# The opening of a time-mix kernel rebuilt, and the rows of its last eight tiles given places of their own

## The chip, the cores and the metric

One Trainium2 chip, one of its cores. The metric is the device time of one execution in microseconds, the median of several.

## What is computed

The reference, cut to what matters: x is (4, 1024, 512), which is 32 tiles of 128 rows, 8 tiles for each batch.

```python
mod = (silu(c) @ wmod).reshape(4, 6, 1, 512)          # c is (4, 512), wmod (512, 3072)
sa, ca, ga, sb, cb, gb = (mod[:, i] for i in range(6))
ga, gb = [(2 * (g >= 0) - 1) * maximum(abs(g), 0.25) for g in (ga, gb)]
h = layernorm(x) * (1 + ca) + sa
# attention part on h: layernorm with ln1, shift by one row, three mixes with mu_r, mu_k, mu_v
r, k, v = sigmoid(xr @ Wr.T), xk @ Wk.T, xv @ Wv.T
h = h + (r * exp(u + k) * v / (exp(u + k) + 1e-8)) @ Wout.T
h = h + sigmoid(xr2 @ Wr2.T) * (square(relu(xk2 @ Wk2.T)) @ Wv2.T)   # second layernorm, shift, mixes
x = x + ga * h
h = layernorm(x) * (1 + cb) + sb
# 8 experts, the best 2 of each row, and a shared one: silu(h @ Wg.T) * (h @ Wu.T) @ Wd.T
x = x + gb * (routed(h) + shared(h))
```

## The kernel before

Each matrix is used as a high part and a low part (`w_r_hi`, `w_r_lo`), and each product of 128 rows and 512 columns is 12 matmuls: four chunks of the inner dimension, by high times high, low times high and high times low. ACT makes the high part of a weight by a copy (`split_hi`), DVE the low part by a subtraction (`split_lo`).

The order is written out by hand for each engine, and semaphores tie the engines together. In the time mix (the first of the two attention parts), step t works on several tiles at once: DVE reads the statistics of x for tile t+4 (`x_stats`), forms h for tile t+3 (`scaled`, `h_of`), normalises tile t+2 (`hhat`) and mixes tile t+1 (`first_col`, `mixes`, `mix_lo`). PE multiplies tile t by r, k and v, turns tile t+2 (`t1`), and from step 2 on turns and multiplies tile t-2 by o. DVE adds that result in `x2_of`. The first steps are -4 to -1, in which PE has nothing of r, k or v to do. POOL forms the reciprocal roots and the difference of neighbouring rows (`diff`). In SP's queue stand the loads of x, the stores of h (`store_h`), and the loads that bring h back. The two places for h are used in turn, so `h_of` of tile n waits until the store of tile n-2 has landed.

Ahead of the time mix stands the opening. PE multiplies silu(c) with the six columns of wmod (24 matmuls, 4 rows each), and each row goes from PSUM to SBUF on DVE, five operations for each gate. The rows are stored to HBM (`store_mod`) and loaded again, spread over 128 partitions, for each batch (`mod1`). The seven weights of the two attention parts pass through three staging buffers and are split, the last three (r2, k2, v2) in the first steps but ahead of tile 0's product.

Behind the attention parts come the experts, in units of 24 matmuls (gate and up, 352 columns) and 9 (down, 512 columns). Units 30 to 37 belong to the shared expert, unit 38 is the first routed one. Rows go to the experts by a scatter of POOL into `expert_in_rows`. SP loads the rows of tiles 24 to 31 for it, writes eight pieces of zeros behind the experts' rows (`pad_rows`, each from the third on waits for the one two before), loads the first two experts' weights (`load_gu`, `load_dn`) and then the first rows (`load_rows`), after all scatters and zeros have landed. PE turns these (`turn_rows(0)`) in unit 37.

## Time and profile before

| | us |
|---|---|
| median of 3 runs | 1725.35 |
| lowest and highest of them | 1723.52, 1727.61 |
| the profiled execution, its own time | 1726.2 |
| span of the profiled execution | 1724.5 |
| PE busy in it | 1642.5 |

The span runs from the first to the last instruction of the core, and the own time of the execution has 1.7 us around it. Times within the trace count from the start of the span. PE is the engine of the matmuls, DVE the vector engine, ACT the scalar engine, POOL the one that scatters, SP the one that issues most transfers. A matmul in the trace lasts longer than the distance to the next one, since they overlap: the distance is what a matmul costs.

### The profile page before, as it was taken

What the parts mean: (1) busy time and instruction counts of PE and PEld (TensorE: products, weight loads), DVE (VectorE), ACT (ScalarE), POOL (GpSimd) and SP (SyncE); (2) the same over time, 40 slices, a digit from 0 to 9 for tenths busy, and PEclk for the clock granted to TensorE, in tenths of its full rate; (3) what the DMA queues carried; (4) which work ended last, traced back from release to release, by engine and by line L of the source; (5) the groups of instructions that cost most, each with busy time, mean ns of one, the idle gap of its engine ahead of it and who ended that gap; (6) DMA issues with size and microseconds to landing.
All of it is one profiled execution on the core that took longest, in us unless ns stands there. A gap on an engine that the chain in (4) does not pass through costs nothing.

```text
span 1724.5 us, 26984 instructions
## 1 busy us (share of the span) xinstructions
PE 1642.5 (95%) x8813; PEld 1429.8 (83%) x8813; DVE 1329.4 (77%) x2559; ACT 766.8 (44%) x1132; POOL 414.3 (24%) x504
## 2 busy tenths in 40 slices
PE   5399999999989999999999997999999999999998
PEld 0278888888768888888888886999999999998897
DVE  4799999998689788888788773777777777775872
ACT  2343333334445555464545422555555555552321
POOL 0243444444222111322232341000000000005740
PEclk9699999999999999999999998999999999999999
DMA  8443232221454434555555687888878988776861
GB/s 327 111 155 98 73 97 79 91 91 67 166 167 146 166 141 141 194 192 196 195 185 177 226 283 260 268 290 283 284 266 277 299 293 282 258 237 194 283 213 37
DMA packets 139121, 335.82 MB, mean 195 GB/s; under 512 B 20584, under 2 KB 20584, under 8 KB 133376
## 3 DMA queue, kind: packets, MB, share of 16 engines
q1 hardware_dynamic: 109328, 248.65, 43.6%
q10 hardware_dynamic: 19440, 52.18, 8.3%
q0 software_dynamic: 10240, 33.56, 5.6%
q8 instruction: 62, 1.02, 0.2%
q14 instruction: 51, 0.42, 0.1%
HBM read 230.73 MB, written 103.60 MB: 194 GB/s over the span
## 4 chain that ended last, share of the span: by engine, by line
PE 78%; DVE 10%; DMA 5%; issue 3%; POOL 2%; ACT 2%; SPq 1%; DVEq 0%; ACTq 0%; POOLq 0%
PE bank L687 19%; PE bank L689 19%; PE bank L688 19%; PE bank L698 5%; PE bank L2321 5%; PE bank L2319 5%; PE bank L2320 5%; PE bank L2314 2%; DMA stage<-in_w_k 1%; DVE mix L1729 1%; POOL raw L1262 1%; DMA expert_in_rows<-y_rows 1%; DVE xm_lo L1735 1%; PE bank L2303 1%; DMA ex_x<-expert_in_rows 1%
## 5 line engine op out<-in xcount | busy, mean ns | idle before, releaser
L687 PE MATMUL bank<-gu_hi,ex_x_hl 128*128 128x352 f32 x1080 | 361.3, 335 | 0.1
L689 PE MATMUL bank<-gu_hi,ex_x_hl 128*128 128x352 f32 x1080 | 350.1, 324 | 0.0
L688 PE MATMUL bank<-gu_lo,ex_x_hl 128*128 128x352 f32 x1080 | 350.1, 324 | 0.0
L1262 POOL DMA_INDIRECT raw<-expert_out_rows,out_slots x64 | 77.1, 1204 | 540.0 <-DMA expert_out_rows<-y_rows 518.2
L687 PEld LDWEIGHTS bank<-gu_hi,ex_x_hl 128*128 128x128 f32 x1080 | 205.1, 190 | 0.4 <-issue 0.3
L688 PEld LDWEIGHTS bank<-gu_lo,ex_x_hl 128*128 128x128 f32 x1080 | 205.1, 190 | 0.0
L689 PEld LDWEIGHTS bank<-gu_hi,ex_x_hl 128*128 128x128 f32 x1080 | 204.7, 190 | 0.0
L1824 DVE TENSOR_TENSOR hid<-bank,sg_t 128x352 f32<-128x352 f32 x135 | 70.4, 521 | 124.8 <-PE bank L689 106.1
L2319 PE MATMUL bank<-dn_hi,hid_hi 128*128 128x512 f32 x405 | 161.3, 398 | 2.4 <-DVE hid_lo L1828 2.4
L2321 PE MATMUL bank<-dn_hi,hid_lo 128*128 128x512 f32 x405 | 159.6, 394 | 0.0
L2320 PE MATMUL bank<-dn_lo,hid_hi 128*128 128x512 f32 x405 | 158.5, 391 | 0.0
L1379 ACT ACTIVATE hid_hi<-bank 128x384 fp32r<-128x384 f32 x135 | 65.3, 484 | 148.8 <-PE bank L2314 148.8
L2090 DVE TENSOR_TENSOR gu_lo<-raw,gu_hi 128x2816 fp32r<-128x2816 f32 x42 | 129.5, 3083 | 1.7 <-ACT gu_hi L1472 1.7
L1828 DVE TENSOR_TENSOR hid_lo<-bank,hid_hi 128x384 fp32r<-128x384 f32 x135 | 74.5, 552 | 70.5 <-ACT hid_hi L1379 70.2
L1472 ACT ACTIVATE gu_hi<-raw 128x2816 fp32r<-128x2816 f32 x42 | 107.6, 2562 | 43.9 <-PE bank L689 43.9
L1476 ACT ACTIVATE dn_hi<-raw 128x1536 fp32r<-128x1536 f32 x42 | 62.5, 1489 | 127.5 <-PE bank L2321 127.5
L1319 ACT ACTIVATE h2T<-bank,vecs 128x128 f32<-128x128 f32 x128 | 48.1, 458 | 155.0 <-PE bank L698 155.0
L687 PE MATMUL bank<-w_r_hi,xm_hi 128*128 128x512 f32 x256 | 104.8, 409 | 11.4 <-DVE h1T L1654 10.3
L687 PE MATMUL bank<-w_k_hi,xm_hi 128*128 128x512 f32 x256 | 104.9, 410 | 0.0
L1663 DVE SCALAR_TENSOR_TENSOR stage<-diff,vecs,h1T 128x128 f32<-128x128 f32 x384 | 102.9, 344 | 0.0
L688 PE MATMUL bank<-w_r_lo,xm_hi 128*128 128x512 f32 x256 | 101.8, 398 | 0.0
L689 PE MATMUL bank<-w_r_hi,xm_lo 128*128 128x512 f32 x256 | 101.6, 397 | 0.0
(256 smaller groups left out, 3826.3 us busy)
## 6 DMA issues: line engine op xcount, KB each, us to landing
raw<-in_ex_gu SPq DMA_DIRECT2D x40, 1408.0 KB, 6.5
raw<-in_ex_dn SPq DMA_DIRECT2D x40, 512.0 KB, 4.9
ex_x<-expert_in_rows SPq DMA_DIRECT2D x71, 256.0 KB, 6.2
expert_out_rows<-y_rows ACTq DMA_DIRECT2D x71, 256.0 KB, 5.9
h_rows<-h_t SPq DMA_DIRECT2D x64, 256.0 KB, 2.6
h_turned<-h_hl ACTq DMA_DIRECT2D x32, 512.0 KB, 3.0
ex_x_hl<-h_turned ACTq DMA_DIRECT2D x32, 512.0 KB, 3.9
x_t<-in_x SPq DMA_DIRECT2D x32, 256.0 KB, 2.7
```

What stands on the lines that cost most here:

```text
L687: pe.matmul(acc, act_hi[i], w_hi[i], start=(i == 0), stop=False)
L688: pe.matmul(acc, act_hi[i], w_lo[i], start=False, stop=False)
L689: last = pe.matmul(acc, act_lo[i], w_hi[i], start=False, stop=(i == chunks - 1))
L698: last = pe.transpose(bank[:, c * P:(c + 1) * P], rows[:, c * P:(c + 1) * P], ident[:])
L1262: pool.indirect_dma_start(rows[:, pair % 2, a, :], None, ys_d, bass.IndirectOffsetOnAxis(ap=out_slots[:, k, n:n + 1], axis=0)).then_inc(ar ...
L1472: act.activation(flat(gu_hi[j % 2][:]), raw[j % 2][:, 0:C * GU], ACT.Copy).then_inc(rw_hi_act.sem, 1)
L1663: last = dve.scalar_tensor_tensor(mix1[:, m, c, :], diff1[:, c, :], vecs[:, mu, c:c + 1], h1T[:, t.p, c, 0:P], ALU.mult, ALU.add)
L1828: dve.tensor_tensor(flat(hid_lo[:]), PS_H[:, 0:FK * P], flat(hid_hi[:]).bitcast(F32), ALU.subtract).then_inc(u_vec.sem_of["hid_lo"], 1)
L2090: dve.tensor_tensor(flat(w_lo[j % 2][:]), raw[j % 2][:, cols], flat(w_hi[j % 2][:]).bitcast(F32), ALU.subtract).then_inc(rw_lo_vec.sem, 1)
L2319: pe.matmul(PS_Y[:], hid_hi[:, c, :], dn_hi[w][:, c, :], start=start and c == 0, stop=False)
L2320: pe.matmul(PS_Y[:], hid_hi[:, c, :], dn_lo[w][:, c, :], start=False, stop=False)
L2321: last = pe.matmul(PS_Y[:], hid_lo[:, c, :], dn_hi[w][:, c, :], start=False, stop=stop and c == FK - 1)
```

## The change

The opening is put together in another way. The product of ones (1 x 128) with the first batch's row of SA and of CA spreads these over the partitions in PSUM, and ACT copies both to `mod1`; only batches 1 to 3 go by HBM. Rows of SA, CA, SB and CB are copied by ACT, and the two gates are formed by four operations of DVE each, in steps 1 and 3. A weight is loaded into the place of its own low part (`weight_in`), so no staging buffer has to come free. Splits of r and k come ahead of everything, v's in step -2, o's in step 0, and r2, k2 and v2 in steps 5, 8 and 11. The nine vectors are loaded from ACT's queue, and the first two tiles of x are loaded near the front of SP's. PE's products for SB, CB and GB stand in steps -2 and -1. On the other side, rows of tiles 24 to 31 all have places in `base`, the second half of the zeros goes behind the first expert's weights, the second expert's weights behind the first rows, and `turn_rows(0)` behind the gate and up of unit 37.

```diff
...
         for w in W2:
-            hi[w], lo[w] = w2_shelf.put(f"w_{w}_hi", [P, C, D], F32R), w2_shelf.put(f"w_{w}_lo", [P, C, D], F32R)
+            hi[w] = w2_shelf.put(f"w_{w}_hi", [P, C, D], F32R)
+            weight_in[w] = Shelf(nc, w2_shelf.at).put(f"w_{w}_in", [P, C, D])
+            lo[w] = w2_shelf.put(f"w_{w}_lo", [P, C, D], F32R)
...
+        mod_home = Shelf(nc, first.at)
+        sa_rows, ca_rows = mod_home.put("sa_rows", [P, D]), mod_home.put("ca_rows", [P, D])
...
+        LAST_HOME = {24: 7, 25: 8, 26: 0, 27: 1, 28: 2, 29: 3, 30: 5, 31: 6}
+
         def last_rows(n):
 
-            return base[:, n - 26, :] if n < 30 else sc_rows[:, n % 2, :]
+            return base[:, LAST_HOME[n], :]
...
+        MOD_BANK = {SA: psum[0], CA: psum[1], GA: psum[3], SB: psum[4], CB: psum[5], GB: psum[7]}
+        MOD_TURN = {SA: 1, CA: 2, GA: 5, SB: 6, CB: 7, GB: 8}
+        SPREAD_TURN = {SA: 3, CA: 4}
+        MOD_COPIED = {SA: 1, CA: 2, SB: 5, CB: 6}
+        SPREAD = psum[6:8]
+        SPLIT_IN_STEP = {-4: ["r", "k"], -2: ["v"], 0: ["o"], 5: ["r2"], 8: ["k2"], 11: ["v2"]}
+        GATE_IN_STEP = {1: GA, 3: GB}
+        SPLITS_DONE = 12
...
             sp.dma_start(cT[:], io["cT"].rearrange("(c p) b -> p c b", p=P)).then_inc(c_in, 16)
+            sp.dma_start(x_t[:, 0, :], x_d[0:P, :]).then_inc(x_in[0], 16)
             load_wmod(0)
-            load_weight(0)
-            load_weight(1)
+            load_weight("r")
+            load_weight("k")
+            sp.dma_start(x_t[:, 1, :], x_d[P:2 * P, :]).then_inc(x_in[1], 16)
             load_wmod(1)
+            load_weight("v")
             load_wmod(2)
-            for t in range(2):
-                sp.dma_start(x_t[:, t, :], x_d[t * P:(t + 1) * P, :]).then_inc(x_in[t], 16)
-
-            store_mod(0)
-            store_mod(1)
-            for i in range(2, len(W1)):
-                load_weight(i)
-            sp.wait_ge(mod_out, 32)
-            for b in range(B):
-                sp.dma_start(flat(mod1[:, b]), mod_d[b, 0:2 * D].partition_broadcast(P)).then_inc(mod1_in, 16)
-            for m in range(2, 6):
-                store_mod(m)
-            for i in range(len(W1), NW - 1):
-                load_weight(i)
+            load_weight("o")
+            sp.dma_start(u_bc[:], io["u"].partition_broadcast(P)).then_inc(u_in, 16)
+            for m in (SA, CA):
+                sp.wait_ge(mod_act, MOD_COPIED[m])
+                store_mod(m, mod_out)
             sp.wait_ge(*lnh_vec.done(0, "scaled"))
             sp.dma_start(x_t[:, 0, :], x_d[2 * P:3 * P, :]).then_inc(x_in[0], 16)
-            sp.dma_start(u_bc[:], io["u"].partition_broadcast(P)).then_inc(u_in, 16)
-            sp.dma_start(wrt[:], io["wrT"].rearrange("(c p) e -> p c e", p=P)).then_inc(vec_in, 16)
...
+            sp.wait_ge(mod_out, 32)
+            for b in range(1, B):
+                sp.dma_start(flat(mod1[:, b]), mod_d[b, 0:2 * D].partition_broadcast(P)).then_inc(mod1_in, 16)
+
+            def later_mod(t):
+
+                if t.only(0):
+                    sp.wait_ge(mod_act, MOD_COPIED[CB])
+                    store_mod(SB, mod_out)
+                    store_mod(CB, mod_out)
+                    sp.wait_ge(mod_mm, MOD_TURN[GB])
+                    for w in W2:
+                        load_weight(w)
...
             wait_a2(sp)
-            for n in range(24, 26):
-                load_scattered(n)
-            for n in range(26, 30):
+            for n in range(24, NT):
                 load_last_scattered(n)
...
             for e in range(E // 2):
                 pad_rows(e)
-            for n in range(30, NT):
-                sp.wait_ge(sc_out[n % 2], 32 * 13)
-                load_last_scattered(n)
-            for e in range(E // 2, E):
-                pad_rows(e)
             sp.wait_ge(raw_pad, 2)
             sp.wait_ge(route_done, 1)
             load_gu(0)
             load_dn(0)
+            for e in range(E // 2, E):
+                pad_rows(e)
             for n in range(FU + 2, SPLIT):
                 load_residual(n)
-            sp.wait_ge(route_vec, SHIFTS_AT)
-            load_gu(1)
-            load_dn(1)
 
...
             sp.wait_ge(h3T_out, 16 * NT)
             for p in range(2):
                 sp.wait_ge(pad_out[p], 16 * (E // 2))
-                sp.wait_ge(sc_out[p], 32 * 13)
-            sp.wait_ge(sc_last_out, 32 * (NT - 26))
-
-            for k in range(3):
+                sp.wait_ge(sc_out[p], 32 * 12)
+            sp.wait_ge(sc_last_out, 32 * (NT - 24))
+
+            for k in range(2):
                 load_rows(k)
+            sp.wait_ge(route_vec, SHIFTS_AT)
+            load_gu(1)
+            load_dn(1)
+            load_rows(2)
...
+            def split_hi(w):
+                act.wait_ge(*weight_arrived(w))
+                act.activation(flat(hi[w][:]), flat(weight_in[w][:]), ACT.Copy).then_inc(wsplit_hi, 1)
+
...
+            def first_batch(m):
+                act.wait_ge(mod_mm, SPREAD_TURN[m])
+                act.activation(mod1[:, 0, m, :], SPREAD[m][:], ACT.Copy).then_inc(mod_act, 1)
+
             act.wait_ge(c_in, 16)
             act.activation(cT[:], cT[:], ACT.Silu).then_inc(silu_c, 1)
...
+            for i in (G1, B1, MUR, MUK, MUV):
+                load_vector(i)
+            split_hi("r")
+            mod_row(SA)
+            split_hi("k")
+            mod_row(CA)
+            for m in (SA, CA):
+                first_batch(m)
+            act.wait_ge(vec_in, 80)
+            for i in (G2, B2, MUR2, MUK2):
+                load_vector(i)
+            act.dma_start(wrt[:], io["wrT"].rearrange("(c p) e -> p c e", p=P)).then_inc(vec_in, 16)
+
+            def opening(t):
+
+                if t.only(-2):
+                    split_hi("v")
+                if t.only(-1):
+                    mod_row(SB)
+                    mod_row(CB)
+                    split_hi("o")
+                for step, weights in SPLIT_IN_STEP.items():
+                    if step > 0 and t.only(step - 1):
+                        for w in weights:
+                            split_hi(w)
...
-                if u == ROUTED0 - 1:
-                    routed_x_hi(0)
                 for piece in HI_FIRST[u]:
                     expert_hi(*piece)
...
+            routed_x_hi(0)
...
+            def split_lo(w):
+                dve.wait_ge(wsplit_hi, split_at(w))
+                dve.tensor_tensor(flat(lo[w][:]), flat(weight_in[w][:]), flat(hi[w][:]).bitcast(F32),
                                   ALU.subtract).then_inc(wsplit_lo, 1)
 
-            def mod_row(m):
-                dve.wait_ge(mod_mm, m + 1)
-                step = MOD_AT[m - 1] if m else 0
...
-            SA, CA, GA, SB, CB, GB = range(6)
-            split_lo(0)
-            split_lo(1)
-            mod_row(SA)
-            mod_row(CA)
-            mod_row(GA)
-            split_lo(2)
-            mod_row(SB)
-            mod_row(CB)
-            mod_row(GB)
-            split_lo(3)
+            def gate_row(m):
+
+                bank, rows = MOD_BANK[m][0:B, :], mod_rows[m]
+                step = GATE_OPS * (m == GB)
+                dve.wait_ge(mod_mm, MOD_TURN[m])
+                if m == GB:
+                    dve.wait_ge(mod_out, 80)
+                    dve.wait_ge(mod_vec, GATE_OPS)
+                dve.tensor_scalar(rows, bank, 0.0, 2.0, ALU.is_ge, ALU.mult).then_inc(mod_vec, 1)
+                dve.tensor_scalar(gate_size, bank, -1.0, 0.25, ALU.mult, ALU.max).then_inc(mod_vec, 1)
+                dve.wait_ge(mod_vec, step + 2)
+                dve.tensor_tensor(gate_size, bank, gate_size, ALU.max).then_inc(mod_vec, 1)
+                dve.wait_ge(mod_vec, step + 3)
+                dve.scalar_tensor_tensor(rows, rows, -1.0, gate_size, ALU.add, ALU.mult).then_inc(mod_vec, 1)
+                dve.wait_ge(mod_vec, step + 4)
...
+            def opening(t):
+
+                if t.pair is not None:
+                    return
+                for w in SPLIT_IN_STEP.get(t.offset, ()):
+                    split_lo(w)
+                if t.offset in GATE_IN_STEP:
+                    gate_row(GATE_IN_STEP[t.offset])
+                if t.only(-1):
+                    dve.wait_ge(u_in, 16)
+                    dve.tensor_scalar(u_bc[:], u_bc[:], LN_1E8, None, ALU.add).then_inc(u_ready, 1)
...
+                if t.only(0):
+                    dve.wait_ge(mod_act, SPREAD_TURN[CA])
+                elif t.only(TPB):
+                    dve.wait_ge(mod1_in, 16 * (B - 1))
...
+            _, _, first_stages = in_turn(
+                (first_col, -1), (hhat, -2), (scaled, -3), (h_of, -3), (h_stats, -3), (h_moments, -3),
+                (x_stats, -4), (x_moments, -4), (mixes, -1), (mix_lo, -1))
+
+            def time_step(t):
+                if t.pair is None and t.offset < 0:
+                    first_stages(t)
+                else:
+                    later_stages(t)
+                opening(t)
...
+            for m in (SA, CA):
+                mod_product(m)
+            for m in (SA, CA):
+                pe.wait_ge(mod_act, MOD_COPIED[m])
+                pe.matmul(SPREAD[m][:], ones_row, mod_rows[m][0:1, :], start=True, stop=True).then_inc(mod_mm, 1)
+            mod_product(GA)
+
+            def opening(t):
+
+                if t.only(-2):
+                    mod_product(SB)
+                if t.only(-1):
+                    mod_product(CB)
+                    pe.wait_ge(mod_act, SPREAD_TURN[CA])
+                    mod_product(GB)
...
-                elif u == ROUTED0 - 1:
-                    turn_rows(0)
                 turn_hid(u - 1)
                 up(u)
+                if u == ROUTED0 - 1:
+                    turn_rows(0)
```

On DVE the first rows of the program were these (weights' low parts, rows of the modulation, then the statistics of the first tiles):

```order
L1554 TENSOR_TENSOR w_r_lo<-stage_95,w_r_hi 128x2048 [waits wsplit_hi]
L1554 TENSOR_TENSOR w_k_lo<-stage_96,w_k_hi 128x2048 [waits wsplit_hi]
L1571 TENSOR_SCALAR h_t<-bank 4x512 [waits mod_mm] x2
L1563 TENSOR_SCALAR xh<-bank 4x512 [waits mod_vec,mod_mm]
L1564 TENSOR_SCALAR diff_90<-bank 4x512
L1566 TENSOR_SCALAR xh<-xh 4x512 [waits mod_vec]
L1567 TENSOR_TENSOR diff_90<-bank,diff_90 4x512
L1569 TENSOR_TENSOR hh<-xh,diff_90 4x512 [waits mod_vec]
```

From step -2 to the mixing of tile 0 in step -1 they are now these:

```order
L1658 BN_STATS st_111<-x_t 128x6 [waits x_in0]
L763 COPY bridge_col<-eps 128x1 [waits lnx_vec]
L1662 BN_AGGR mv_112<-st_111 128x2
L1618 TENSOR_TENSOR w_v_lo<-w_v_in,w_v_hi 128x2048 [waits wsplit_hi]
L1705 TENSOR_TENSOR h1T<-h1T,keep 128x4
L1699 TENSOR_SCALAR hh<-h_t,mv1h,rstd1h 128x512 [waits lnh_pool]
L1672 SCALAR_TENSOR_TENSOR xh<-x_t,mv_112,mod_94 128x512 [waits lnx_vec]
L1683 SCALAR_TENSOR_TENSOR h_t<-xh,rstd_113,mod_94 128x512 [waits lnh_vec,lnx_pool,h_out0]
L1689 BN_STATS st1h<-h_t 128x6 [waits lnh_vec]
```

The rows of the modulation have left DVE's front. Tile 0's mixing stands behind the statistics of tile 2's x and behind tile 2's h, which waits for the store of tile 0's h (`h_out0`).

In SP's queue, at the way into the routed part, there stood this after the first four pieces of zeros:

```order
L987 DMA sc_rows<-h_rows 128x512 x2
L1025 TENSOR_LOAD pad_row
L1025 ISA x2
L1026 ISA
L1026 DMA expert_in_rows<-y_rows 128x512
```

There stands this now, in which the first expert's weights precede the fifth piece of zeros:

```order
L766 DMA raw_188<-in_ex_gu 128x2816
L771 ISA
L771 DMA raw_188<-in_ex_dn 128x2x512
L773 ISA
L773 DMA raw_188<-in_ex_dn 96x512
L1049 TENSOR_LOAD pad_row
L1049 ISA x2
L1050 ISA
L1050 DMA expert_in_rows<-y_rows 128x512
```

On PE the first routed rows were turned ahead of unit 36's turn (`hid`) and unit 37's 24 matmuls of gate and up:

```order
L2321 MATMUL bank<-dn_hi,hid_lo 128x512
L698 MATMUL bank<-ident,ex_x 128x128 [waits ex_in0]
L698 MATMUL bank<-ident,ex_x 128x128 x3
L2314 MATMUL bank<-ident,hid 128x128 [waits u_vec_hid,u_vec_hid_lo]
L2314 MATMUL bank<-ident,hid 128x128 x2
L687 MATMUL bank<-gu_hi,ex_x_hl 128x352 [waits u_vec_hid]
```

They are turned now behind the last of these 24 and ahead of unit 36's down:

```order
L703 MATMUL bank<-gu_hi,ex_x_hl 128x352
L712 MATMUL bank<-ident,ex_x 128x128 [waits ex_in0]
L712 MATMUL bank<-ident,ex_x 128x128 x3
L2410 MATMUL bank<-dn_hi,hid_hi 128x512 [waits u_vec_hid_lo,base_vec]
L2411 MATMUL bank<-dn_lo,hid_hi 128x512
```

## Rows read from the trace of the kernel before

**Rows 1.** The page of the profile, engines' busy time, share of the span and instructions.

```profile
PE 1642.5 (95%) x8813; PEld 1429.8 (83%) x8813; DVE 1329.4 (77%) x2559; ACT 766.8 (44%) x1132; POOL 414.3 (24%) x504
```

**Rows 2.** Waits of PE: who waited for what, us in total, times, longest.

```profile
PE bank L698 <- DVE hh L1648: 20.4, 1, 20.4
PE bank L698 <- DMA ex_x<-expert_in_rows: 12.2, 1, 12.2
...
PE bank L687 <- DVE h1T L1654: 10.3, 2, 9.6
PE bank L698 <- ACT h1T L1284: 6.3, 1, 6.3
```

**Rows 3.** Timeline of PE, opening: start, us, engine, line, operation, tiles, count.

```profile
9.40 9.88 PE L2194 MATMUL bank<-wmod,cT 128*4 128x512 f32 x16 [9.40 <-DMA wmod<-in_wmod]
20.62 13.90 PE L2194 MATMUL bank<-wmod,cT 128*4 128x512 f32 x32 [1.34 <-DMA wmod<-in_wmod]
...
73.10 0.76 PE L687 MATMUL bank<-w_r_hi,xm_hi 128*128 128x512 f32 x1 [9.64 <-DVE h1T L1654]
...
105.32 0.40 PE L687 MATMUL bank<-w_r_hi,xm_hi 128*128 128x512 f32 x1
```

**Rows 4.** Chain that ended last, opening, transfers: start us, us, what.

```profile
4.04 11.42 DMA stage<-in_w_k
...
21.22 8.55 DMA stage<-in_w_v
```

**Rows 5.** Windows (busy per engine, PEclk, DMA share, GB/s) of the vector loads.

```profile
42.00:56.00 14.00, 1.05 (x4) 0.72 (x4) 9.97 (x17) 3.82 (x2) 2.13 (x7) 0.50 0.76 176
```

**Rows 6.** Timeline of DVE, opening, idle time in brackets.

```profile
24.25 0.68 DVE L1563 TENSOR_SCALAR xh<-bank 4x512 f32<-4x512 f32 x1 [3.35 <-PE bank L2194]
...
50.68 2.29 DVE L1554 TENSOR_TENSOR w_k_lo<-stage,w_k_hi 128x2048 fp32r<-128x2048 f32 x1 [2.28 <-ACT w_k_hi L1275]
...
60.23 0.69 DVE L1609 BATCH_NORM_STATS2 st<-x_t 128x6 f32<-128x512 f32 x1 [3.70 <-DMA x_t<-in_x]
...
66.41 3.24 DVE L1663 SCALAR_TENSOR_TENSOR stage<-diff,vecs,h1T 128x128 f32<-128x128 f32 x12
...
71.20 1.76 DVE L1669 TENSOR_TENSOR xm_lo<-stage,xm_hi 128x1536 fp32r<-128x1536 f32 x1 [0.67 <-ACT xm_hi L1292]
72.87 0.16 DVE L1654 TENSOR_TENSOR h1T<-h1T,keep 128x4 f32<-128x4 f32 x1
...
82.39 0.16 DVE L1654 TENSOR_TENSOR h1T<-h1T,keep 128x4 f32<-128x4 f32 x1
...
92.97 0.15 DVE L1654 TENSOR_TENSOR h1T<-h1T,keep 128x4 f32<-128x4 f32 x1
...
103.84 0.15 DVE L1654 TENSOR_TENSOR h1T<-h1T,keep 128x4 f32<-128x4 f32 x1
```

**Rows 7.** Timeline of DVE, ten tile steps later.

```profile
224.66 0.15 DVE L1654 TENSOR_TENSOR h1T<-h1T,keep 128x4 f32<-128x4 f32 x1
```

**Rows 8.** Waits of DVE, 112 to 400 us.

```profile
DVE hin_t L1694 <- PE bank L689: 18.5, 24, 0.9
```

**Rows 9.** Timeline of PE where the routed part begins.

```profile
1051.63 0.39 PE L2321 MATMUL bank<-dn_hi,hid_lo 128*128 128x512 f32 x1
1064.18 1.11 PE L698 MATMUL bank<-ident,ex_x 128*128 128x128 f32 x4 [12.17 <-DMA ex_x<-expert_in_rows]
...
1070.04 0.32 PE L687 MATMUL bank<-gu_hi,ex_x_hl 128*128 128x352 f32 x1
...
1071.47 0.39 PE L2319 MATMUL bank<-dn_hi,hid_hi 128*128 128x512 f32 x1
```

**Rows 10.** Timeline of SP's queue, the same place.

```profile
1052.83 1.45 SPq L1063 DMA_DIRECT2D ex_x<-expert_in_rows  x2
```

**Rows 11.** Transfers, 1015.25 to 1064.2 us, all queues.

```profile
DMA packets 5941, 15.64 MB, mean 320 GB/s; under 512 B 752, under 2 KB 752, under 8 KB 5682
```

**Rows 12.** Transfers of rows of zeros, 1037 to 1046 us: count, KB, us to landing.

```profile
expert_in_rows<-y_rows SPq DMA_DIRECT2D x4, 256.0 KB, 3.5
```

More of the change, by code:

```diff
@@ L236, in put, with time_mix @@
         return tensor
-def time_mix(eng, lead, lag, body):
-    low = lag + 2 + lag % 2
+def time_mix(eng, lead, lag, body, low=None):
+    low = low or lag + 2 + lag % 2
     high = min(NT - lead, JOIN) // 2 * 2
@@ L545, in build @@
         u_in = sem("u_in")
-        w_in = [sem(f"w_in{i}") for i in range(3)]
+        w_in = [sem(f"w_in{i}") for i in range(len(W1))]
         mod_out = sem("mod_out")
@@ L1245, in scatter_last @@
                                             last_rows(n), None).then_inc(sc_last_out, 16)
-            for n in range(24, 26):
-                scatter(n)
-            for n in range(26, NT):
+            for n in range(24, NT):
                 scatter_last(n)
@@ new lines, in opening @@
+            def opening(t):
[9 more added lines that the diff above has]
+                            split_hi(w)
+                if t.only(SPLITS_DONE - 2):
+                    act.wait_ge(vec_in, 160)
+                    act.activation(wrt_hi, wrt[:], ACT.Copy).then_inc(wsplit_hi, 1)
@@ L2187, in _, with mod_product @@
         def _(pe):
-            pe.wait_ge(silu_c, 1)
-            for m in range(6):
-                if m % 2 == 0:
-                    pe.wait_ge(wmod_in[m // 2], 16 * C)
+            def mod_product(m):
+                pe.wait_ge(wmod_in[m // 2], 16 * C)
                 for c in range(C):
-                    last = pe.matmul(psum[m][0:B, :], cT[:, c, :], wmod[:, c, m * D:(m + 1) * D], start=(c == 0),
+                    last = pe.matmul(MOD_BANK[m][0:B, :], cT[:, c, :], wmod[:, c, m * D:(m + 1) * D], start=(c == 0),
                                      stop=(c == C - 1))
                 last.then_inc(mod_mm, 1)
+            pe.wait_ge(silu_c, 1)
             pe.wait_ge(const_ready, CONSTS)
-            pe.wait_ge(mod_vec, MOD_DONE)
+            for m in (SA, CA):
[11 more added lines that the diff above has]
+                    mod_product(GB)
             def t1(t):
@@ L2212, in r @@
                     pe.wait_ge(*sr_act.done(t.back(1).n, "sr"))
-                if t.pair is None and t.n == 0:
-                    pe.wait_ge(wsplit_lo, NW + 1)
+                if t.only(0):
+                    pe.wait_ge(wsplit_lo, split_at("r"))
                 pe.wait_ge(*mix_vec.done(t.n, "mix_lo"))
```

148 lines of the change are left out of this document (72 added, 76 removed).

## The prediction

> **What bounds the kernel now.** I read the page first: PE is busy for 1642.5 of the 1724.5 us [rows 1], so the kernel is bound by PE, and a change pays by what it takes out of PE's 82 us of idle time, or puts into it. PE's waits come next [rows 2]. The reader is to see that few waits hold most of it: 20.4, 6.3 and 9.6 us in the opening, and one of 12.2 us for the first routed rows. PE's timeline gives the opening its size: tile 0's first product starts at 73.10 us, 9.40 us being the arrival of wmod [rows 3]. Until 34.5 us PE has only the modulation's products. Behind 105.32 us (tile 3) the tile steps follow at (224.66 - 103.84) / 10 = 12.08 us [rows 6, 7]. In them DVE waits for PE once a step, 18.5 / 24 = 0.77 us [rows 8], so a step costs DVE 11.31 us: it is nearly as loaded as PE. DVE's last part of tile 3's mixing ends at 103.84 us, 1.48 us before PE takes it. That is all the lead that it has.
>
> **The opening: when tile 0's product can start.** In the new order the chain is set by arrivals. k, with 4.2 MB issued up to its end, landed at 4.04 + 11.42 = 15.46 us, and v, with 9.95 MB, at 21.22 + 8.55 = 29.77 us [rows 4]. That is 0.402 MB a microsecond, in order of issue. Now 11.3 MB (x, wmod, four weights, u) stand ahead of the stores of the rows SA and CA: 15.46 + 7.1 / 0.402 = 33.1 us. To this come the vectors from ACT's queue. In the 14 us in which all nine and the router's weights were loaded, transfers were busy for 0.76 x 14 = 10.6 us and moved 176 x 14 = 2.46 MB, which takes 6.1 us [rows 5]. The other 4.5 us are the ten small loads', and five of them come early: 2.3 us. The stores land at 35.4 us.
>
> The spreading itself is done well ahead. SA's and CA's products took 9.9 us from wmod's arrival [rows 3], and this comes 2.9 us later (x 0.7, vectors 2.2). ACT's copies and the two products with ones, which no row shows, are bounded by nothing and by 0.9 us each (two records of 0.434 us, 13.90 / 32 in [rows 3], for a wmod matmul of as many columns). So DVE scales tile 0 at about 24 us. But x of tile 2, issued then, stands behind the same 11.3 MB and lands at about 36 us, and DVE has its statistics ahead of tile 0's mixing. Then SP waits for the stores, issues `mod1` of three batches (1.57 MB, 3.9 us) and only then the store of tile 0's h, some 2.6 us: 41.9 us. DVE's h of tile 2 waits for that store. From there to the end of tile 0's mixing: h, two statistics and their moments, 2.2 us (0.69 for a pass of 512, less overlap); the mixes 3.24; ACT's high part, 71.20 - 69.65 = 1.55; the low part 1.67 [rows 6]. Sum 8.7, so tile 0 starts at **50.6 us** instead of 73.1. PE's CB and GB products, in step -1, start at about 41 us and take another 9.9 us if PE is slow again as in its first two: 50.8. They end together with it, and so cost nothing here.
>
> **What is moved into the steps.** DVE's steps without waits were 82.39 - 72.87 = 9.5, 10.6 and 10.9 us [rows 6] for tiles 1 to 3, and are 11.31 behind. Added are 0.4 (u) for tile 1; o's low part, 2.3, for tile 2; gate GA, four operations of 0.65, 2.6, for tile 3; GB, 2.6, for tile 5; r2, k2 and v2, 2.3 each [rows 6], for tiles 7, 10 and 13. A tile's product starts at the later of two times: 12.08 us after the one before (8.8 for tiles 1 and 2), and when DVE is done. DVE itself is at least 10.7 us behind the start of the tile before, since it waits for PE's o. Walked through: tile 1 at 60.6, tile 2 at 73.5, tile 3 at 87.0, tile 4 at 99.1 (PE's own pace), tile 5 at 112.2, tile 6 at 124.3, tile 7 at 137.1, tile 8 at 149.2, tile 9 at 161.3, tile 10 at 173.5, tile 12 at 197.7, tile 13 at 210.0. Before, tile 13 starts at 105.32 + 10 x 12.08 = 226.1. So of the 22.5 us of an earlier start 6.4 are given back, nearly all up to tile 5: with three steps between, a split of 2.3 us is just won back by three waits of 0.77. Gain **16.1 us**. ACT's splits (1.9 us each) lie in its idle time: it is busy for 766.8 us of the span [rows 1]. Its wait, however, is in front of v's in step -2 only.
>
> **The way into the routed part.** PE ended unit 35's down at about 1051.86 us and began unit 36's at 1071.47: 19.6 us [rows 9]. Of this, 12.2 are the wait, and the gate and up behind it ran at first at half clock. With rows in time the same work is a turn (0.33), 24 matmuls at (1071.47 - 1070.04) / 9 = 0.16, and the turn of the rows (0.44): 4.6 us. That is 15.0 us less. The rows are now wanted at 1051.86 + 4.2 = 1056.0. Are they there? They were issued at 1052.83 [rows 10] behind the second expert's 1.97 MB, and landed at 1064.2. In the 49 us up to then 15.64 MB moved, 320 GB/s in the mean [rows 11]. Without the second expert's weights and second rows 13.4 MB are needed: at 320 they land at 1057.1, at 402 at 1048.6. By the chain: scatters, which need not wait for a place to come free, end at about 1041; the zeros' third pair waits behind the first expert's weights until about 1042.5, the fourth takes 3.5 us [rows 12], to 1047; then rows in some 4 us: 1051. I take 1051, no wait; the bound is 1.1 us of wait. DVE does the low part of the first gate and up (about 3 us) before that of the rows, and PE's next turn waits some 0.3 us more for it. Gain **14.7 us**.
>
> The Trainium skill (DMA: Bandwidth & Descriptors, Queues, rings and completion order) says that each transfer engine takes the queues that have work in turn, packet by packet. By this rule POOL's scatters would keep half of each engine, the 1.97 MB would take 9.8 us instead of 4.9, and all zeros behind them, and the rows, would come 5 us later, at 1056: the gain would be the same or a microsecond less. Before, no row shows the two queues against each other.
>
> **Sum.** 1726.2 - 16.1 - 14.7 = 1695.4 in the profiled execution's terms. It lies 0.85 above the median of 1725.35, so **1694.5 us**. Unknowns: tile 0's start from 45 (x and the store land as on an empty queue, at DVE's own pace) to 55 (they wait twice for the vectors and `mod1`), 6 us down and 5 up; five moved pieces on DVE, if POOL's work beside them stretches each by 0.7 us, 3 up; the routed entry 0.5 down to 6 up. In all 1688 to 1707.
>
> **Rivals.** (A) Both gains as above, chance 0.75. (B) The opening gives little, 1703 us, chance 0.11: DVE does not win back its delay. The moved pieces (14.8 us with u's) are then paid in full: from 50.6 us at PE's pace tile 13 would start at 201.1, with the 2.5 us that PE lost before tile 3 in the old order too, and these 14.8, at 218.4, and the opening's gain is 7.7. For it speaks that the margin is as good as none: three waits of 0.77 against 2.3. Against it, that the 0.77 us stood in all 24 steps. (C) The routed wait stays for the most part, 1706 us, chance 0.08: zeros, fourfold in a row by their own waits, land 12 us later behind the weights, as 1.97 MB and the scatters share the engines. For it speaks the busy queue [rows 11]; against it the 13.4 MB. (D) Slower than before, chance 0.03: PE's short waits in steps 1 to 13 keep it at half clock. [Rows 5] show it granted 0.50 in a stretch in which it had worked 1 of 14 us. At 0.43 instead of 0.23 us a matmul a step is 9.5 us longer, and from four such steps on the kernel is slower: ten would give 1790. Against it: no wait in my walk is longer than 4 us, against 20.4 before. (E) The change does nothing, chance 0.03: other transfers make both waits anew, 1725.
>
> **Range and chances.** The 8 in 10 range is 1686 to 1707; it takes in (A) and the better part of (B) and (C). A measurement of this kernel tells about 0.2%, 3.5 us, from no change. Faster: 0.75 + 0.11 + 0.08 = 0.94. The same 0.03, slower 0.03.
>
> **What would show it.** In the new trace: tile 0's first product with r at 50.6 us; DVE waiting before the statistics of tile 2's x until about 36 us and before tile 2's h until about 42; PE waits of 3 us and less in tiles 1 to 3, 5 and 7, none behind tile 13; tile 13 at 210; no wait for the first routed rows, and PE at full clock there. It is wrong if tile 0 starts later than 55, if PE waits in each step from 5 to 12, or if the routed rows land behind 1057 less the opening's gain.

## The result

The changed kernel takes 1698.72 us (median of four runs, 1697.35 to 1702.0) against 1726.48 for the kernel before beside it: ratio 0.9846, 95% interval 0.9828 to 0.9863. The forecast was 1694.5 us, with a range of 1686 to 1707. The profiled execution of the changed kernel took 1702.0 us, the longest of its four runs and 24.2 less than that of before; the medians lie 27.8 apart, and a part of that difference has a cause, below.

The page of the changed kernel, span and engines' busy time, answers to [rows 1]. PE is busy as long as before (1643.6 against 1642.5 us), so the gain is idle time:

```profile
span 1700.3 us, 26873 instructions
PE 1643.6 (97%) x8817; PEld 1426.7 (84%) x8817; DVE 1326.2 (78%) x2553; ACT 770.3 (45%) x1138; POOL 417.9 (25%) x505
```

PE's waits answer to [rows 2]. The first three are of the opening (the third is in front of the products of tiles 0, 1 and 2), the fourth is of the tile steps behind it, and the last two are of the way into the routed part:

```profile
PE bank L2255 <- DMA wmod<-in_wmod: 11.9, 2, 10.3
PE bank L712 <- DVE hh L1699: 11.4, 2, 10.1
PE bank L701 <- DVE xm_lo L1720: 6.0, 3, 3.7
...
PE bank L701 <- DVE rw_lo L1741: 2.2, 4, 0.9
...
PE bank L2410 <- DVE hid_lo L1892: 2.7, 1, 2.7
PE bank L712 <- DVE ex_x_hl L2147: 0.7, 1, 0.7
```

The wait of 12.2 us for the first routed rows is gone; a new one of 2.7 us stands behind it. PE's timeline answers to [rows 3]: tile 0's, tile 2's and tile 13's first product with r, then unit 36's and unit 37's down (start, us, engine, line, tiles, in brackets the idle time before and what ended it):

```profile
52.46 0.47 PE L701 MATMUL bank<-w_r_hi,xm_hi 128*128 128x512 f32 x1 [1.57 <-DVE xm_lo L1720]
...
75.06 0.47 PE L701 MATMUL bank<-w_r_hi,xm_hi 128*128 128x512 f32 x1 [3.65 <-DVE xm_lo L1720]
...
212.50 0.40 PE L701 MATMUL bank<-w_r_hi,xm_hi 128*128 128x512 f32 x1
...
1043.35 0.48 PE L2410 MATMUL bank<-dn_hi,hid_hi 128*128 128x512 f32 x1
...
1053.94 0.50 PE L2410 MATMUL bank<-dn_hi,hid_hi 128*128 128x512 f32 x1 [2.71 <-DVE hid_lo L1892]
```

In the trace of before, the same product of tile 13 and the downs of units 35 and 37 start here, and unit 36's down at 1071.47 us [rows 9]:

```profile
225.86 0.40 PE L687 MATMUL bank<-w_r_hi,xm_hi 128*128 128x512 f32 x1
...
1049.78 0.39 PE L2319 MATMUL bank<-dn_hi,hid_hi 128*128 128x512 f32 x1
...
1079.44 0.51 PE L2319 MATMUL bank<-dn_hi,hid_hi 128*128 128x512 f32 x1 [1.14 <-DVE hid_lo L1828]
```

So the changed kernel is ahead by 20.6 us at tile 0, 13.4 at tile 13, still 13.2 at unit 35's down, 28.1 at unit 36's and 25.5 at unit 37's. From unit 39 on it is 23.8, and 24.2 at the end. Such leads, always over the one trace of the kernel before, are how all traces below are read. The opening of the changed kernel stands word for word in five traces, and its lead at tile 17 is 13.35, 13.21, 13.10, 12.71 and 12.07 us in them. So a difference of about a microsecond between two leads says nothing.

### The profile page after: what moved, and what is told of

It reads as the page before. It is cut to its first block, busy times and chain, and to the rows that moved or that the text cites. A ratio compares the mean times of both kernels' runs of the same rounds, so it can differ in the third digit from the quotient of the medians.

```text
span 1700.3 us, 26873 instructions
## 1 busy us (share of the span) xinstructions
PE 1643.6 (97%) x8817; PEld 1426.7 (84%) x8817; DVE 1326.2 (78%) x2553; ACT 770.3 (45%) x1138; POOL 417.9 (25%) x505
## 4 chain that ended last, share of the span: by engine, by line
PE 73%; DVE 15%; DMA 4%; issue 3%; SPq 2%; ACT 2%; POOL 1%; DVEq 0%; ACTq 0%; POOLq 0%
PE bank L701 17%; PE bank L703 17%; PE bank L702 17%; PE bank L712 5%; PE bank L2412 5%; PE bank L2410 5%; PE bank L2411 5%; PE bank L2405 2%; DVE stage L1714 2%; DVE mix L1793 1%; DVE xm_lo L1799 1%; DMA expert_in_rows<-y_rows 1%; SPq L798 1%; DMA mod_rows<-ca_rows 1%; PE bank L2394 1%
## 5 line engine op out<-in xcount | busy, mean ns | idle before, releaser
L1892 DVE TENSOR_TENSOR hid_lo<-bank,hid_hi 128x384 fp32r<-128x384 f32 x135 | 74.4, 551 | 60.7 <-ACT hid_hi L1445 60.6
```

What stands on the lines that cost most here:

```text
L1892: dve.tensor_tensor(flat(hid_lo[:]), PS_H[:, 0:FK * P], flat(hid_hi[:]).bitcast(F32), ALU.subtract).then_inc(u_vec.sem_of["hid_lo"], 1)
```

## Experiments

Each kernel was timed beside the kernel before, whose median was 1725.74 us in the runs of the first four experiments, 1728.53 in the next four, 1725.8 in the next three and 1729.49 in the last. A ratio given beside a median is not the quotient of the two medians; it lies up to 0.0018 beside it, which is 3 us.

### The two halves of the change apart

One kernel has the old opening and the new way into the routed part; the other has the opposite. In the second these lines are put back:

```diff
+            for n in range(30, NT):
+                sp.wait_ge(sc_out[n % 2], 32 * 13)
+                load_last_scattered(n)
+            for e in range(E // 2, E):
+                pad_rows(e)
             sp.wait_ge(raw_pad, 2)
             sp.wait_ge(route_done, 1)
             load_gu(0)
             load_dn(0)
-            for e in range(E // 2, E):
-                pad_rows(e)
```

Expected of the routed part alone: 

> The kernel before with only the part on the way into the routed experts changed. From the pair of traces I read that this part shortens the way to unit 36's down by 14.9 us and then gives 4.3 us back in units 37 and 38, so on the whole 10.6 us: 1715.8 us against 1726.4, ratio 0.9939. Theory of the prediction: 14.7 us stay, 1711.7 us. Rival, that the two parts depend on each other (the rows are in time only because the opening moved everything against the transfers): under 8 us.

Expected of the opening alone: 

> The changed kernel with the way into the routed experts put back as before, so the opening alone. By the tile starts in the pair of traces the gain is 13.4 us: 1713.0 us, ratio 0.9923. The prediction's walk gives 16.1 us (1710.3). Rival B of the prediction, in which the delay of DVE is never won back, gives 7.7 us (1718.7). The wait for the first routed rows is 12 us again.

Measured: the routed part alone 1717.01 us, ratio 0.9933 (0.9909 to 0.9958), the opening alone 1710.81, ratio 0.9898 (0.9873 to 0.9922). By the traces the first gains 14.5 us from unit 35's to unit 36's down and gives 5.6 back in units 37 and 38; the second leads by 13.2 us at tile 17 and by 13.8 at unit 40. With the old opening PE waits only 0.3 us for the first routed rows, so their being in time does not hang on the new one. The two gains add up to 23.7 us by the medians and to 29.2 by the ratios, against 27.8 and 26.6 for the whole change: within what such runs tell, the halves do not depend on each other. The opening gives far more than rival B's 7.7 us.

### Where 4.3 us are lost in units 37 and 38

ACT's timeline of the changed kernel shows what unit 37's down waited for. ACT stands at the copy of the second expert's gate and up until the transfer has landed, and the high part of unit 37 is queued behind it:

```profile
1049.66 2.56 ACT L1538 ACTIVATE gu_hi<-raw 128x2816 fp32r<-128x2816 f32 x1 [2.41 <-DMA raw<-in_ex_gu]
1052.12 0.57 ACT L1531 ACTIVATE ex_x_hl<-bank 128x512 fp32r<-128x512 f32 x1
1052.59 0.48 ACT L1445 ACTIVATE hid_hi<-bank 128x384 fp32r<-128x384 f32 x1
```

Windows of the changed kernel (us, busy time of PE, PEld, DVE, ACT and POOL, granted clock, DMA share, GB/s) show the second part of the loss. Ahead of 1053.94 us PE had worked 1.24 of 3.94 us. In the stretch behind it the granted clock was 0.64 in the mean; it was still full up to 1055 us and 0.50 from 1056 to 1058:

```profile
1050.00:1053.94 3.94, 1.24 (x9) 0.95 (x7) 1.21 (x3) 3.43 (x4) 0.00 (x0) 1.00 1.00 382
1053.94:1058.50 4.56, 4.56 (x17) 3.85 (x18) 4.46 (x4) 1.41 (x2) 0.00 (x0) 0.64 1.04 310
```

The chain that ended last, in the changed kernel, says why the transfer is late. The fifth piece of zeros took 12 us, and only then could the seventh and eighth, the rows and the second expert's weights be issued. The last line is the down part of these weights; the gate and up for which ACT stood were issued 1.1 us ahead of it, at 1041.79 us:

```profile
1022.71 12.01 DMA expert_in_rows<-y_rows
...
1036.54 2.06 DMA expert_in_rows<-y_rows
...
1042.90 9.14 DMA raw<-in_ex_dn
```

Two edits attack the two ends of this. The first lets ACT make that copy behind unit 37's high part:

```diff
-            hi_first[u].append((j + 1, "gu"))
+            (hi_first if j else hi_middle)[u].append((j + 1, "gu"))
```

Expected: 

> The changed kernel, in which ACT makes the high part of the second expert's gate and up behind the rows' and unit 37's high parts, not ahead of them. Theory 1: unit 37's down waits 2.71 us only because ACT stands at this copy for a transfer until 1049.66 us; then the wait goes, PE does not fall to half clock at 1055 us, and the kernel is 4.3 us faster than the changed one, 1694.4 us. Theory 2: the clock falls for another reason (the turns and the 0.73 us wait): 2.7 us faster, 1696.0, half clock still there. Theory 3: DVE's low parts are what is late: under 1 us.

The second puts all eight pieces of zeros ahead of the first expert's weights:

```diff
-            for e in range(E // 2):
+            for e in range(E):
                 pad_rows(e)
...
             load_dn(0)
-            for e in range(E // 2, E):
-                pad_rows(e)
```

Expected: 

> The changed kernel, with the second four pieces of zeros issued ahead of the first expert's weights, as before the change. Theory 1: the fifth zeros took 12.0 us because they stood behind 1.97 MB that got half of the transfer engines beside the scatters; now all zeros are landed by 1025 us, the rows are issued by about 1033 instead of 1039.5, the second expert's weights land by 1045 instead of 1052, unit 37's down waits at most the 1.1 us that it waited before, PE keeps full clock: about 3.5 us faster, 1695.2 us. Theory 2: the second expert's weights are slow on their own (rows of the next units beside them), whatever is ahead: no gain, 1698.7. Theory 3: the first expert's weights come too late for ACT's copy at 1039.65 us: slower.

Measured: 1698.4 us (ratio 0.9824, 0.9803 to 0.9846) and 1698.1 (0.9829, 0.9808 to 0.985). The totals are 4.0 and 2.9 us above what was expected; the ratios lie 0.0022 and 0.0017 below the changed kernel's, 3.8 and 2.9 us, within intervals that are wider than that. The totals alone cannot tell 4 us, the traces can tell where it went: from unit 35's down to unit 39 the first gains 15.3 us on before and the second 15.0, against 10.6 in the changed kernel's trace (and 13.75 in another of the changed kernel, below, so the edits are worth 1.3 to 4.7 us). In both, PE's only wait between 1030 and 1075 us is this one, the clock is 1.00 in every window of that stretch, and in the second the rows are issued at 1031.71 instead of 1039.54 us. From the trace with the zeros first, PE's wait and the issue of the rows in SP's queue, then from the one with ACT's order the copy:

```profile
PE bank L712 <- DVE ex_x_hl L2145: 0.9, 1, 0.9
1031.71 1.47 SPq L1077 DMA_DIRECT2D ex_x<-expert_in_rows  x2
...
1049.16 2.56 ACT L1538 ACTIVATE gu_hi<-raw 128x2816 fp32r<-128x2816 f32 x1
```

So the mechanism of theory 1 holds in both. With ACT's order alone, the copy still starts only at 1049.16 us, yet nothing waits: half clock was a consequence of the wait, not a cause of its own.

### How DVE pays for the moved pieces

The splits of r2, k2 and v2 in a row instead of three steps apart:

```diff
-        SPLIT_IN_STEP = {-4: ["r", "k"], -2: ["v"], 0: ["o"], 5: ["r2"], 8: ["k2"], 11: ["v2"]}
+        SPLIT_IN_STEP = {-4: ["r", "k"], -2: ["v"], 0: ["o"], 5: ["r2"], 6: ["k2"], 7: ["v2"]}
```

Expected: 

> The changed kernel with the splits of r2, k2 and v2 in steps 5, 6 and 7, not 5, 8 and 11. Own theory: DVE can be late by about 1.65 us before PE stalls (2.3 us of a split cost 0.65), and wins back 0.77 us a step. With three steps between, each costs 0.65: 1.95 in all. In a row the second and third cost 1.5 each: 3.7 in all, so tile 13 starts 1.7 us later than in the changed kernel (offset of 11.7 us to before instead of 13.4) and the kernel is 1.7 us slower. Rival B of the prediction (nothing is won back, each piece is paid in full wherever it stands): tile 13 starts at the same time.

Their low parts in halves, one each in steps 5, 7, 9, 11, 13 and 15:

```diff
+        LOW_HALVES = {5: ("r2", 0), 7: ("r2", 1), 9: ("k2", 0), 11: ("k2", 1), 13: ("v2", 0), 15: ("v2", 1)}
...
+                part = slice(2 * half, 2 * half + 2)
+                op = dve.tensor_tensor(flat(lo[w][:, part, :]), flat(weight_in[w][:, part, :]),
```

Expected: 

> The changed kernel with DVE's low parts of r2, k2 and v2 made in halves of 1.15 us, one each in steps 5, 7, 9, 11, 13 and 15 (ACT's high parts in steps 5, 9 and 13, whole). Own theory: 1.15 us is less than the 1.65 us that DVE can be late, and two steps win back 1.54, so no half stalls PE: tile 17 starts 1.95 us earlier than in the changed kernel. Rival 1: what stalls PE there is ACT's copy of 1.9 us, not DVE: no gain. Rival 2: every piece is paid in full: no gain.

Tile 17's first product with r starts here, in the trace of before, of the changed kernel, of the splits in a row and of the halves:

```profile
274.07 0.40 PE L687 MATMUL bank<-w_r_hi,xm_hi 128*128 128x512 f32 x1
...
260.72 0.40 PE L701 MATMUL bank<-w_r_hi,xm_hi 128*128 128x512 f32 x1
...
262.79 0.40 PE L701 MATMUL bank<-w_r_hi,xm_hi 128*128 128x512 f32 x1
...
259.30 0.40 PE L701 MATMUL bank<-w_r_hi,xm_hi 128*128 128x512 f32 x1
```

Lead over before at tile 5 and at tile 17, so what the three splits cost, each within one trace: the changed kernel 15.4 and 13.35, a loss of 2.03; in a row 14.6 and 11.3, a loss of 3.28; in halves 14.77 and 14.77, none. Three steps apart the pieces of 2.28 us cost 0.63, 0.65 and 0.75; in a row the first costs 0.65 and the two behind it 1.3 each; and a piece of 1.21 us costs nothing. So DVE wins back about 1.0 us a step (2.28 less 1.3), somewhat more than the 0.77 that it was seen to wait; but what it can be late by in all is some 1.65 us (2.28 less 0.63), however many steps lie before the piece. The copies on ACT are free. Rival B is refuted. The totals of these two, and of the next two, are not comparable (1720.74 and 1714.49 us): a stop in another place covers them, told below.

### What sets tile 0's start

The loads of o and u behind the stores of SA and CA and tile 2's x, and `mod1` of batches 1 to 3 behind the store of tile 1's h:

```diff
-            load_weight("o")
-            sp.dma_start(u_bc[:], io["u"].partition_broadcast(P)).then_inc(u_in, 16)
             for m in (SA, CA):
...
             sp.dma_start(x_t[:, 0, :], x_d[2 * P:3 * P, :]).then_inc(x_in[0], 16)
-            sp.wait_ge(mod_out, 32)
-            for b in range(1, B):
+            load_weight("o")
+            sp.dma_start(u_bc[:], io["u"].partition_broadcast(P)).then_inc(u_in, 16)
```

Expected: 

> The changed kernel with the loads of o and u behind the stores of the rows SA and CA and the load of tile 2's x, and mod1 of batches 1 to 3 behind the store of tile 1's h. Own theory (SP's transfers land in the order of their issue at 0.402 MB/us): 1.31 MB less stand ahead, so x of tile 2 is there 3.3 us earlier, at about 32.5 us; the store of tile 0's h no longer waits for the stores to land and lands at about 37 instead of 43.25; h of tile 2 follows. Tile 0's product then starts when PE has ended the CB and GB products behind tile 1's turn, about 48 to 49 us instead of 52.5. Rival: tile 0's start is set by DVE's own order and the weights' splits, not by arrivals: 52 us, no gain. For the whole kernel 2 to 4 us less, if steps 1 to 3 do not give it back.

The same with PE's product for GB in step 1, and the loads of r2, k2 and v2 in step 2:

```diff
                     mod_product(CB)
+                if t.only(1):
                     pe.wait_ge(mod_act, SPREAD_TURN[CA])
                     mod_product(GB)
```

Expected: 

> The same, and PE's product for GB (4 us) moved from step -1 to step 1, the loads of r2, k2 and v2 to step 2. Own theory: GB's product is then hidden in the 3.65 us that PE waits in front of tile 2's product, and tile 0 starts when DVE has its mixing: about 46 us. Since DVE sets tiles 0 to 3 either way, 1 to 3 us less than the run before at tile 5. Rival: PE is then late for tile 2, and what tile 0 wins is lost there: the same as the run before.

The first starts tile 0 at 50.05 us, not at 48 to 49, and leads by 15.77 at tile 17, 2.4 more than the changed kernel, where 2 to 4 were expected. In a second run (below) it started tile 0 at 50.30 and led by 14.35, against 13.1 for the changed kernel beside it, so the gain is 1.3 to 2.4 us, and the lower end is no more than the changed kernel's own leads differ by. DVE's timeline of that second run has x of tile 2 at 32.0 us, as the order of issue gave (32.5), and then a new wait:

```profile
32.02 0.69 DVE L1661 BATCH_NORM_STATS2 st<-x_t 128x6 f32<-128x512 f32 x1 [1.60 <-DMA x_t<-in_x]
...
36.71 2.29 DVE L1621 TENSOR_TENSOR w_v_lo<-w_v_in,w_v_hi 128x2048 fp32r<-128x2048 f32 x1 [3.72 <-ACT w_v_hi L1299]
```

The second edit loses: tile 0 at 49.94 us and not at 46, since DVE has its mixing ready no sooner, and a lead of only 10.3 at tile 17. Its trace shows two things that I had not priced. Without GB's product PE stood idle for 4.43 us ahead of tile 0 and did most of its product with r at half clock, 0.43 us a matmul instead of 0.23. And in SP's queue `hin_t` stood behind 3.1 MB of weights; DVE waited 5.75 us for it, and the lead fell from 19.1 us at tile 3 to 14.1 at tile 4 and 12.3 at tile 5. That is nearly the whole loss:

```profile
49.94 0.47 PE L701 MATMUL bank<-w_r_hi,xm_hi 128*128 128x512 f32 x1 [4.43 <-DVE xm_lo L1723]
...
50.99 0.63 PE L701 MATMUL bank<-w_r_hi,xm_hi 128*128 128x512 f32 x1
...
52.27 0.63 PE L701 MATMUL bank<-w_r_hi,xm_hi 128*128 128x512 f32 x1
...
92.11 0.69 DVE L1750 TENSOR_TENSOR hin_t<-bank,hin_t 128x512 f32<-128x512 f32 x1 [5.75 <-DMA hin_t<-h_rows]
```

### A stop that comes and goes with one and the same kernel, and the edits together

The four runs before this one were on one chip, and all came out some 18 us or more above what was expected (1720.74, 1714.49, 1714.72 and 1719.24 us). The same kernels were then run on another:

Expected of the changed kernel again: 

> The changed kernel, word for word, run once more beside the next two. In the four runs ahead of this the tile starts did what was expected, but each trace has a new stop of ACT, DVE and PE of 10 to 12 us between 1006 and 1026 us, beside the scatters, and up to 9 us more near 1560 to 1620 us, beside the gathers. Theory 1: it belongs to the chip on which those four ran. Then on that chip the changed kernel shows it too (1712 to 1720 us), and on another one none of the three shows it (1699). Theory 2: it belongs to those kernels' order of instructions; then this one is at 1699 us wherever it runs, and the next one shows the stop again.

Expected of the one with o behind the stores: 

> The kernel with the loads of o and u behind the stores, word for word as in the run of that name. Tile 0 at 50 us again, tile 17 2.4 us earlier than in the changed kernel. Theory 1 (the chip): without the stop it is 2.4 us faster than the changed kernel beside it, and has the stop only if that one has it too. Theory 2 (the kernel's order): the stop of 10 to 12 us at the scatters is there again, 1711 to 1715 us.

Expected of all four edits: 

> The changed kernel with four edits at once: low parts in halves, o and u behind the stores, the second four pieces of zeros ahead of the first expert's weights, and ACT's copy of the second expert's weights behind unit 37's high part. If they add up: 1.4 + 2.4 us at tile 17 and 4.3 us at unit 38, 8.1 us less than the changed kernel beside it, 1690.5 us. If the stop is one of the kernel's order, it may be there: then 1700 to 1705.

Measured: the changed kernel 1699.19 us (ratio 0.9851, 0.9834 to 0.9867), the one with o behind the stores 1695.79 (0.9832, 0.9815 to 0.985), all four edits **1693.6** (0.9815, 0.9799 to 0.9831). The second is word for word the kernel that took 1714.72. ACT's timeline and the window of 1006 to 1026 us, first in its run on the first chip, then in that on the other:

```profile
1025.71 0.49 ACT L1448 ACTIVATE hid_hi<-bank 128x384 fp32r<-128x384 f32 x1 [18.97 <-remote]
1006.00:1026.00 20.00, 8.68 (x50) 7.53 (x48) 6.56 (x25) 0.76 (x2) 13.63 (x14) 0.84 0.71 272
```

```profile
1006.00:1026.00 20.00, 19.46 (x112) 17.64 (x111) 17.60 (x56) 2.98 (x7) 15.08 (x16) 1.00 0.96 339
```

On the first chip ACT and DVE stop beside the last scatters, and PE then waits for DVE's `hid_lo`. The turn that ACT's copy needs ended on PE at 1010.95 us, 14.8 us ahead of the copy; POOL's last scatter instruction ended at 1023.68, 2.0 us ahead of it. In the pair the order of instructions is the same, so theory 2 is refuted for it. Theory 1 is only half tested: the changed kernel never ran on the first chip, and the kernel before, whose time is only 2.7 us longer there (1728.53 against 1725.8), has no trace there. So whether the stop takes the chip alone, or the chip and a kernel changed in this way, or something else that differed between the two occasions, is open.

The second run of the changed kernel also explains part of the 24.2 against 27.8 us. There the second expert's weights landed at 1047.6 us instead of 1049.7, ACT waited 1.12 us instead of 2.41, unit 37's down 1.3 instead of 2.7, and PE kept full clock (1.00 in every stretch of that part): 13.75 us gained on the way into the routed part instead of 10.6. One or two microseconds of a late transfer decide over three.

All four edits together lead by 18.35 us at tile 17 and by 35.08 at unit 100, 7.5 more than the changed kernel beside them (27.54), nearly the 8.1 expected. In part that is luck: 5.3 of it stand at tile 17, where 3.8 were expected, and 2.3 come in the routed part, where 4.3 were. And the total is 1693.6 us, 5.6 less than the changed kernel's and not 8.1, for 3.7 are lost behind 1530 us, where PE's waits for `hid` are 5.1 us instead of 3.0 before. Nearly all of it goes between the downs of units 120 and 130. There the kernel with the zeros first alone loses 2.1 us, the four edits 3.5 and the five 3.45, and no other kernel more than 1.5. These three have the zeros first in common; no run takes that edit out of the four, so that it is the cause is not shown.

Last, the wait for `w_v_hi` above:

```diff
-            for i in (G2, B2, MUR2, MUK2):
-                load_vector(i)
-            act.dma_start(wrt[:], io["wrT"].rearrange("(c p) e -> p c e", p=P)).then_inc(vec_in, 16)
...
+                for step, i in zip((1, 2, 3, 4), (G2, B2, MUR2, MUK2)):
+                    if t.only(step):
+                        load_vector(i)
```

Expected: 

> The kernel with four edits, and a fifth: ACT issues the last four vectors in steps 1 to 4 and the router's weights in step 6, not ahead of step -2. In the trace with four edits ACT stands in the issue of the router's weights (4.7 us) until 33.4 us, and the high part of v and DVE's low part of it, at 36, come late by it. Theory: tile 1's normalised rows, PE's turn and the CB and GB products come 3 to 4 us earlier, and tile 0 starts at 46 to 47 us instead of 49.5; at tile 5 the offset to before is about 21 us instead of 18.35, and the whole is 3 us faster than with four edits, 1690.5. Rival 1: v's own transfer lands only then; no change. Rival 2: the issues in the steps hold ACT up (the router's weights took 4.7 us), and the steps give back what tile 0 wins.

Its opening does this: h1T is formed at 29.09 us, v's high part at 30.48, tile 0 starts at 47.55 (46 to 47 expected), behind CB's and GB's products and at full clock, and the lead at tile 5 and tile 17 is 20.38 us, 2.0 more than with four edits (2.7 expected). ACT's timeline of the kernel with o behind the stores, whose opening ACT works through in the same order, had shown one issue as the brake. It took 4.72 us while transfers kept the 16 engines busy all the time; with five edits the same load, issued at 128.22 us, took 0.38:

```profile
28.61 4.72 ACTq L1323 DMA_DIRECT2D wrt<-in_wrT  x1
33.38 1.50 ACT L1346 ACTIVATE h1T<-bank,vecs 128x128 f32<-128x128 f32 x4 [11.24 <-DMA vecs<-in_ln_g]
```

The total of the fifth edit's kernel, 1709.64 us, ratio 0.9878 (0.9854 to 0.9901), where 1690.5 was expected, came from another chip again, and its trace has the stop, 19.24 us on ACT. So whether it is faster than 1693.6 on a chip without the stop stays open.

## Why the prediction was right, and where it was off

**Arrivals in the opening.** The order of issue at 0.402 MB/us held. Stores of SA and CA landed at 34.9 us (35.4 predicted), tile 2's x at 35.8 (36). From the changed kernel, the chain that ended last, and DVE's waits for x and for the store:

```profile
23.48 11.44 DMA mod_rows<-ca_rows
...
36.34 6.91 DMA h_rows<-h_t
```

```profile
35.81 0.69 DVE L1658 BATCH_NORM_STATS2 st<-x_t 128x6 f32<-128x512 f32 x1 [5.75 <-DMA x_t<-in_x]
...
43.27 0.75 DVE L1683 SCALAR_TENSOR_TENSOR h_t<-xh,rstd,mod 128x512 f32<-128x512 f32 x1 [0.90 <-DMA h_rows<-h_t]
```

The term that was too small is "`mod1` 3.9 us, and the store some 2.6": from the stores' landing to that of tile 0's h it was 8.3 us, not 6.5. From there to tile 0's product it was 9.2 us, not 8.7. So tile 0 started at 52.46 us instead of 50.6; CB's and GB's products ended at 50.9, as said.

**The walk through the tiles** was right up to tile 9. Predicted and measured starts: tile 1 at 60.6 and 62.3, tile 2 at 73.5 and 75.1, tile 4 at 99.1 and 100.9, tile 7 at 137.1 and 138.8, tile 13 at 210.0 and 212.5. The distance stays 1.6 to 1.9 us up to tile 9, and is 2.1 at tile 10 and 2.5 at tile 13. The step that failed is "a split of 2.3 us is just won back by three waits of 0.77": the walk let the second and third split cost some 0.1 and 0.2 us, as if DVE's lead kept growing between them, and they cost 0.65 and 0.75, as much as the first. Of 20.6 us, 7.3 were given back (6.4 predicted). What I also placed wrongly is the wait: behind tile 3 it is in front of o's product (`rw_lo`), not r's, and tile 2's was 3.65 us, not 3 or less. The gain was 13.4 us, not 16.1: 1.9 of the difference are tile 0's start, 0.9 what was given back.

**The way into the routed part.** Unit 36's down came 14.9 us sooner, as predicted (15.0 less 0.3). But the rows had no 5 us to spare; they were issued at 1039.54 and wanted at 1042.94, and PE's load of them as weights waited 0.2 us: in time with nothing over. The step that failed is "the zeros' third pair waits behind the first expert's weights until about 1042.5", in the new trace's time 1029.3: it landed at 1034.7. The transfers between 1020.17 and 1034.73 us in the changed kernel (queue and kind, packets, MB, share of 16 engines; SP's queue, then POOL's) show SP's queue at 2.68 / 14.56 = 0.18 MB/us, not 0.402:

```profile
q1 hardware_dynamic: 812, 2.68, 55.4%
q0 software_dynamic: 574, 1.84, 31.9%
```

The Trainium skill (DMA: Bandwidth & Descriptors, Queues, rings and completion order) has the engines take the queues in turn; the prediction gave 5 us later by that rule, and the trace agrees, with 5.4. The halves were not equal, though: the engines gave 55.4% of their time to SP's queue and 31.9% to POOL's.

And a step is missing from the prediction: I counted the second expert's weights out of the rows' way, and did not ask who waits for them there. ACT does, and through it unit 37's down: 2.7 us and half clock behind it, 4.3 in all in the profiled execution, 1.3 in another.

**The sum** erred by 4.2 us, and the size of two terms is the reason: tile 0's start (1.9) with what is given back (0.9), and units 37 and 38 (1 to 4). The gain itself was 27.8 us against 30.8 forecast; 1.1 of the 4.2 us is the kernel before, whose median was 1726.48 beside the changed one and 1725.35 in the forecast. The worst cases named add up to 1708.5 us (5, 3 and 6 on 1694.5), not 1707, which changes nothing here. Rival B fell with the splits in a row and in halves, rival C with the wait that is gone, rival D with the granted clock, nine tenths of full speed or more in every slice of the page, and rival E with the totals.

## What to carry to other kernels

Work moved into the steps of a loop on an engine that is nearly as loaded as the bound one is free if each piece is smaller than that engine's lead and the spacing lets the slack pay it back: here 1.2 us cost nothing, 2.3 us cost 0.65 or so three steps apart and 1.3 in a row. The lead has a ceiling, so wider spacing does not make the larger piece free. When a transfer is moved behind another to let that one pass, the engine that stands at it in its own order is the next thing to price, with what is queued behind its wait. Before a total is believed, read the lead over the old kernel at named instructions: the leads agreed to about a microsecond where totals differed by twenty.

## What the runs showed of the hardware

In five traces on two chips ACT stood for 16 to 20 us and DVE for 6.5 to 10 beside POOL's scatters, with PE behind them, and the lead fell by 12 to 16 us from unit 30's to unit 34's down. In eight others it fell there by at most 0.8, and in the trace of before ACT stood for 4.4 us at most. One and the same kernel went both ways (1714.72 and 1695.79 us). Beside the gathers near 1560 to 1620 us the four traces of the first of these chips lost 2.6 to 8.8 us more, the fifth 0.2. The kernel before is only 2.7 and 3.7 us slower on those two chips (1728.53 and 1729.49 against 1725.8). Such a stop hides gains of a few microseconds.

Issuing a transfer can cost its engine time: one load of 16 KB took ACT 4.72 us behind four others and beside 16 busy engines, during which ACT computed nothing, and 0.38 us in step 6 of the kernel with five edits.

PE ran at half clock behind a stretch in which it had worked 1.24 of 3.94 us, and behind 4.43 idle us; behind waits of 1.3 and 0.9 us it kept full clock.
